# Layer 1's depthwise convolution in blocks of 4 rows by 28 columns instead of 2 rows by 56

## The chip, the cores and the metric

One core of one Trainium2 chip runs the whole kernel. The metric is device microseconds of one execution, as the median of the runs. Engines are called by the profile's names: PE (TensorE, matmuls), PEld (its weight loads), DVE (VectorE), ACT (ScalarE), POOL (GpSimd), SP (SyncE, which here only issues DMA transfers).

## The reference

Two layers on 32 images of 96 channels, 56 x 56 pixels, float32.

```
# layer 0
h = depthwise_conv(x, conv_w 7x7, pad 3) + conv_b
h = layernorm over the 96 channels, * ln_g + ln_b
h = gelu(h @ w1 + b1) @ w2 + b2            # 96 -> 384 -> 96, per pixel
x = h * layer_scale + x
# layer 1, on x
x = silu(depthwise_conv(x, conv_w 5x5, pad 2) + conv_b);  xs = x as [96, 3136]
dts, Bs, Cs = x_proj_w @ xs                # 6, 4 and 4 rows
delta = softplus(dt_w @ dts + dt_b)
log_dA = max(delta * A, log 1e-9);  P = exp(cumsum(log_dA))        # along the pixels, 4 states
hs = P * cumsum(delta * Bs * xs / max(P, 1e-9))
y = sum over the states(hs * Cs) + xs * Ds
```

## The kernel before

Images are taken in 8 groups of 4. The layers run one after the other; layer 0 writes its result x1 to DRAM, layer 1 reads it from there.

**Convolution as matmuls (both layers).** A padded image lies in `xpad`, channels on partitions. "Turns" transpose windows of it into `win`: a window is a block of whole padded rows, here 2, laid out on the partitions (layer 1: 2 x 60 = 120), and `win` holds it for every channel, image and block row. A block of 2 x 56 = 112 outputs is then a sum over KT windows of (taps matrix) x (window): the taps of one channel are banded matrices, prepared on the host, loaded by DMA as the stationary operand; the moving operand is that channel's 4 images x 28 blocks = 112 columns. Layer 1 has KT2 = 3, so 3 matmuls per channel (two instructions each in the trace, since they are fp32), 24 "conv" units of 4 channels per group, each in two pieces. ACT copies a unit's PSUM bank to `conv`. "Back" units transpose `conv` (pixels on partitions) to 128 rows (32 channels x 4 images) x 448 pixels, 4 transposes of 112 columns each, and ACT applies bias and SiLU into `xs`.

**Layer 0.** While group g goes through normalisation, up and down projections in 28 units of 448 pixels, the windows of g+1 are turned beside it; the convolution of g+1 then runs by itself. The last step of a unit is `residual` (L421): DVE adds `ps_down`, the bias and the original pixels into `x1o`, and SP stores `x1o` to DRAM (L279). PE's `down` two units later waits for `x1_done`.

**Layer 1.** A group has 7 bands of 448 pixels (8 rows), 3 tiles of 128 rows and 4 states: S = 84 steps of one tile and state, 12 to a band. A step on DVE is two scans (L1115, L1140) and a product (L1128). POOL makes `u` (L1040) and multiplies by `c_rows` (L1054), PE sums over the states (L1363), ACT makes `d_a` (L1220, L1226). Beside this, the next band's `delta` is prepared: `project` (L1337), `xd` (L1193), stored to DRAM and read back as `b_rows` and `c_rows`, `delta_rows` (L1350), `z_log` on ACT (L1209, L1211, L1202), `delta` on DVE (L1106).

The next group's turns (L1308, 24 units of 15 transposes) and conv units (L1315) are laid beside the steps by an order written out in `units` and `schedule`: one piece or one turn a step up to step 71, the first eight steps all turns, then conv, conv, turn, and from step 56 only conv. Back units come in bursts at steps 35 (3), 60 (7), 72 (8) and 0 of the next group (3); at a burst ACT loads the SiLU table and, behind it, the old table. All front work takes turns in two PSUM banks, and a unit waits until the one two before it is kept by ACT. Group 0's front work runs ahead of everything ("EARLY"). Every engine's order is that of its program; there is no other planner. SP's queue holds all loads: slabs of x1 (32 channels of one image) into three thirds of `xpad` (L911), taps in three slots (L920), `b_rows`, `c_rows`, stores. Each waits for its slot, and what is behind it in the queue waits too. The groups are iterations of a hardware loop.

## Time and profile before

| | |
|---|---|
| median of 3 runs | 3963.23 us (3962.03 to 3977.51) |
| the profiled execution, its own time | 3967.54 us |
| its span, first to last instruction | 3965.7 us |
| mean granted clock of PE | 0.936 |
| busy: PE, DVE, ACT, POOL | 3632.9, 3026.1, 2572.0, 2459.8 us |
| layer 1's convolution matmuls (L1315) | 4608 instructions |

A row of an engine's groups gives busy time, the mean of one instruction and, behind the bar, the idle time just before them and what ended it. Instructions overlap at their ends, so busy times of neighbours add up to a little more than the time that passes; from start to start is what one costs. "issue" is time in which the engine waited for nothing that the profile shows.

### The profile page before, as it was taken

What the parts mean: (1) busy time and instruction counts of PE and PEld (TensorE: products, weight loads), DVE (VectorE), ACT (ScalarE), POOL (GpSimd) and SP (SyncE); (2) the same over time, 40 slices, a digit from 0 to 9 for tenths busy, and PEclk for the clock granted to TensorE, in tenths of its full rate; (3) what the DMA queues carried; (4) which work ended last, traced back from release to release, by engine and by line L of the source; (5) the groups of instructions that cost most, each with busy time, mean ns of one, the idle gap of its engine ahead of it and who ended that gap; (6) DMA issues with size and microseconds to landing.
All of it is one profiled execution on the core that took longest, in us unless ns stands there. A gap on an engine that the chain in (4) does not pass through costs nothing.

```text
span 3965.7 us, 71069 instructions
## 1 busy us (share of the span) xinstructions
PE 3632.9 (92%) x22358; PEld 2638.3 (67%) x22358; DVE 3026.1 (76%) x3888; ACT 2572.0 (65%) x4292; POOL 2459.8 (62%) x2298
## 2 busy tenths in 40 slices
PE   6999999999999999997899898998989989989876
PEld 6888797978788787877666465664655646556422
DVE  3675748475766758481299899998999989999999
ACT  1463818173654628175688787887887888878865
POOL 0362717163543627171287888878887888888898
PEclk9999999999999999998889898998999989989887
DMA  7546374746555474526566464664656646555322
GB/s 223 170 130 221 95 252 101 250 104 205 143 168 177 114 239 98 185 71 151 138 176 172 128 180 129 173 180 122 186 135 166 174 118 184 151 158 169 100 79 64
DMA packets 383733, 612.75 MB, mean 155 GB/s; under 512 B 199967, under 2 KB 324152, under 8 KB 383048
## 3 DMA queue, kind: packets, MB, share of 16 engines
q1 hardware_dynamic: 383336, 607.74, 54.4%
q8 instruction: 214, 3.51, 0.4%
q14 instruction: 183, 1.50, 0.1%
HBM read 527.35 MB, written 80.28 MB: 153 GB/s over the span
## 4 chain that ended last, share of the span: by engine, by line
PE 40%; issue 6%; ACT 3%; POOL 2%; DVE 2%; DMA 0%; DVEq 0%; ACTq 0%; POOLq 0%
PE ps_front L1315 12%; PE ps_y L1363 12%; PE ps_front L1308 4%; PE ps_prep L1337 4%; PE ps_y L1360 3%; PE ps_prep L1350 3%; PE ps_front L1328 2%; DVE h L1140 1%; POOL h L1054 1%; POOL u L1040 1%; DVE ps_q L1115 1%; ACT win L1177 1%; ACT d_a L1226 1%; ACT xs L1184 1%; POOL dxs L1028 1%
## 5 line engine op out<-in xcount | busy, mean ns | idle before, releaser
L322 POOL TENSOR_TENSOR h_low<-act_h,h_high 128x448 fp32r<-128x448 f32 x448 | 597.7, 1353 | 724.5 <-ACT h_high L521 724.2
L516 ACT ACTIVATE act_h<-ps_up,b 128x448 f32<-128x448 f32 x672 | 408.7, 633 | 728.1 <-PE ps_up L634 727.9
L1054 POOL TENSOR_TENSOR h<-h,c_rows 128x448 f32<-128x448 f32 x672 | 728.1, 1084 | 219.5 <-DVE h L1140 141.2
L1363 PE MATMUL ps_y<-h,ident 128*128 128x448 f32 x1344 | 704.8, 612 | 104.9 <-POOL h L1054 92.0
L1040 POOL TENSOR_TENSOR u<-dxs,b_rows 128x448 f32<-128x448 f32 x672 | 762.1, 1134 | 51.9 <-DMA bc_dram<-xd 37.6
L1115 DVE TENSOR_TENSOR_SCAN ps_q<-d_a,q_last,ps_q 128x450 f32<-128x450 f32 x576 | 661.2, 1148 | 0.2 <-ACT d_a L1226 0.2
L1140 DVE TENSOR_TENSOR_SCAN h<-d_a,h_last,ps_q 128x449 f32<-128x449 f32 x576 | 647.0, 1123 | 0.0
L1315 PEld LDWEIGHTS ps_front<-win,taps 120*112 120x112 f32 x4608 | 537.3, 187 | 143.9 <-issue 140.3
L607 PE MATMUL ps_stage<-win,taps 124*112 124x112 f32 x6144 | 608.2, 261 | 2.7 <-DVE w_low L369 2.7
L607 PEld LDWEIGHTS ps_stage<-win,taps 124*112 124x112 f32 x6144 | 607.9, 178 | 3.2 <-DVE w_low L369 2.8
L1220 ACT ACTIVATE d_a<-delta,log_eps,a_neg 128x448 f32<-128x448 f32 x672 | 503.4, 750 | 71.8 <-DVE h L1140 52.9
L1315 PE MATMUL ps_front<-win,taps 120*112 120x112 f32 x4608 | 542.5, 271 | 7.1 <-ACT win L1177 3.7
L1363 PEld LDWEIGHTS ps_y<-h,ident 128*128 128x128 f32 x1344 | 230.8, 202 | 373.2 <-POOL h L1054 207.7
L427 DVE TENSOR_TENSOR conv<-ps_stage,bias_row 112x448 f32<-112x448 f32 x192 | 179.6, 935 | 350.8 <-PE ps_stage L607 350.8
L1128 DVE SCALAR_TENSOR_TENSOR ps_q<-ps_q,u 128x449 f32<-128x449 f32 x672 | 409.4, 609 | 42.3 <-POOL u L1040 42.0
L1226 ACT ACTIVATE d_a<-d_a 128x448 f32<-128x448 f32 x672 | 388.3, 578 | 8.3
L316 POOL TENSOR_TENSOR ln_rstd<-ln_var,minus_half 112x7 f32<-112x7 f32 x128 | 202.7, 1583 | 285.4 <-DVE ln_var L404 281.2
L1177 ACT ACTIVATE conv<-ps_front 112x448 f32<-112x448 f32 x192 | 182.3, 949 | 215.4 <-PE ps_front L1315 215.4
L630 PE MATMUL ps_up<-hn_high,w_high 96*128 96x448 f32 x672 | 259.0, 385 | 38.1 <-DVE hn_low L414 24.9
L1308 PEld LDWEIGHTS ps_front<-ident,x1pad 32*120 32x120 f32 x2880 | 190.0, 138 | 135.1 <-issue 133.4
L1028 POOL TENSOR_TENSOR dxs<-delta,xs 128x448 f32<-128x448 f32 x168 | 190.9, 1136 | 139.5 <-DVE delta L1106 139.5
L1106 DVE SCALAR_TENSOR_TENSOR delta<-ps_prep,z_log 128x448 f32<-128x448 f32 x168 | 103.6, 617 | 216.3 <-ACT z_log L1202 210.4
(83 smaller groups left out, 6190.8 us busy)
## 6 DMA issues: line engine op xcount, KB each, us to landing
taps<-in_t_dram SPq DMA_DIRECT2D x192, 896.0 KB, 5.1
taps<-in_t_dram SPq DMA_DIRECT2D x192, 672.0 KB, 4.7
b_rows<-bc_dram SPq DMA_DIRECT2D x224, 224.0 KB, 3.0
c_rows<-bc_dram SPq DMA_DIRECT2D x224, 224.0 KB, 3.2
xres<-in_x_dram SPq DMA_DIRECT2D x224, 168.0 KB, 2.5
x_dram<-x1o SPq DMA_DIRECT2D x224, 168.0 KB, 2.0
x1pad<-x_dram SPq DMA_DIRECT2D x96, 392.0 KB, 5.8
out_dram<-y SPq DMA_DIRECT2D x168, 224.0 KB, 2.5
```

The lines of the kernel that those rows point to most:

```text
L322: nc.gpsimd.tensor_tensor(h_low[u % 2][:, t, :], act_h[u % 2][:, t, :], h_high[u % 2][:, t, :], ALU.subtract).then_inc(h_low_ready[t], 1)
L516: nc.scalar.activation(act_h[u % 2][:, t, :], ps_up[t][:, 0:BT], ACT.Gelu, bias=b1[:, t:t + 1]).then_inc(gelu_done, 1)
L607: mm = nc.tensor.matmul(ps_stage[q % 2][0:TOK, c * BLOCKS:(c + 1) * BLOCKS], taps[q % SLOTS1][0:WIN1, c, k, :], win[:, q * CQ + c, :, k:k ...
L1040: nc.gpsimd.tensor_tensor(u[s % U_SLOTS][:, 0:BT], dxs[:, t, :], b_rows[n][:, :], ALU.mult).then_inc(u_done, 1)
L1054: nc.gpsimd.tensor_tensor(total, total, c_rows[n][:, :], ALU.mult).then_inc(hc_done, 1)
L1115: nc.vector.tensor_tensor_scan(q_bank(s, BT + 2), d_a[s % DA_SLOTS][:, :], no_q.broadcast_to([128, BT + 2]), q_first[:, 0:1] if b == 0 els ...
L1128: nc.vector.scalar_tensor_tensor(q_bank(s, BT + 1), q_bank(s, BT + 1), 1.0, u[s % U_SLOTS][:, :], ALU.min, ALU.mult).then_inc(gated, 1)
L1140: nc.vector.tensor_tensor_scan(h[:, s % H_SLOTS, :], d_a[s % DA_SLOTS][:, 0:BT + 1], q_bank(s, BT + 1), first, ALU.mult, ALU.add).then_inc ...
L1220: nc.scalar.activation(d_a[s % DA_SLOTS][:, 0:BT], delta[:, t, :], ACT.Relu, bias=log_eps[:, 0:1], scale=a_neg[:, t, n:n + 1]).then_inc(cl ...
L1226: nc.scalar.activation(d_a[s % DA_SLOTS][:, 0:BT], d_a[s % DA_SLOTS][:, 0:BT], ACT.Exp, bias=LOG_EPS).then_inc(d_a_ready, 1)
L1315: mm = nc.tensor.matmul(bank[i][0:TOK, c * BLOCKS:(c + 1) * BLOCKS], taps[n % SLOTS2][0:WIN2, c, w, :], win[cb % 2][:, k * CQ + c, :, w:w ...
L1363: nc.tensor.matmul(total, ident[:, :], h[:, s % H_SLOTS, 0:BT], start=False, stop=(n == N - 1)).then_inc(y_added, 1)
```

## The change

A block of layer 1's convolution becomes 4 rows x 28 columns, still 112 outputs. It is read from a padded half image of 32 columns, so a window is 4 x 32 = 128 values, and two windows (KT2 = 2) hold the 8 rows that 5 taps over 4 rows need. `win` has the same size: 15 windows for each of two halves instead of 30. The moving operand is 4 images x 2 halves x 14 block rows. The halves overlap by the columns that both need; layer 0 writes both, with the zeros at the image's left and right edge, so x1 in DRAM has shape [images x channels, 2, 56, 32], and a slab load copies whole rows. Turns: still two per image, 15 transposes each, of 128 columns instead of 120. Back units: still 4 transposes, their results woven together by rows of 28. The host makes other taps (`patched`), 448 KB a load instead of 672.

```diff
-COLS2 = W + 2 * PAD2
-WIN2 = ROWS * COLS2
-KT2 = (ROWS + K2 - 1) // ROWS
-NWIN2 = (H + 2 * PAD2) // ROWS
+PATCH_ROWS, PATCH_COLS = 4, W // 2
+PCOLS = PATCH_COLS + 2 * PAD2
+SEEN = PCOLS - PAD2
+WIN2 = PATCH_ROWS * PCOLS
+KT2 = (PATCH_ROWS + K2 - 1) // PATCH_ROWS
+ROW_BLK = H // PATCH_ROWS
+ROW_WIN = (H + 2 * PAD2) // PATCH_ROWS
+NWIN2 = 2 * ROW_WIN
+BAND_ROWS = BT // W
+BAND_BLK = BAND_ROWS // PATCH_ROWS
...
-        x1o = [sb(f"x1o{i}", [C, BT]) for i in range(2)]
+        x1o = [sb(f"x1o{i}", [C, 2, BAND_ROWS, PCOLS]) for i in range(2)]
...
-                sp.wait_ge(x1_done, g * UNITS + u + 1)
-                sp.dma_start(x1[ds((g * GI + u // BANDS) * C, C), (u % BANDS) * BT:(u % BANDS + 1) * BT],
-                             x1o[u % 2][:, :]).then_inc(x1_stored[u % 2], 16)
+                sp.wait_ge(x1_done, (g * UNITS + u + 1) * 2)
+                rows = slice(u % BANDS * BAND_ROWS, (u % BANDS + 1) * BAND_ROWS)
+                sp.dma_start(x1[ds((g * GI + u // BANDS) * C, C), :, rows, :].rearrange("c f h w -> c f (h w)"),
+                             x1o[u % 2][:, :, :, :].rearrange("c f h w -> c f (h w)")).then_inc(x1_stored[u % 2], 16)
...
+            for i in range(2):
+                nc.gpsimd.memset(x1o[i][:, 0, :, 0:PAD2], 0.0).then_inc(prepared, 1)
+                nc.gpsimd.memset(x1o[i][:, 1, :, SEEN:PCOLS], 0.0).then_inc(prepared, 1)
...
-                nc.vector.scalar_tensor_tensor(x1o[u % 2][:, :], ps_down[u % 2][0:C, 0:BT], b2[:, 0:1],
-                                               xres[u % 2][:, :], ALU.add, ALU.add).then_inc(x1_done, 1)
+                total = ps_down[u % 2][0:C, 0:BT].rearrange("c (h w) -> c h w", w=W)
+                res = xres[u % 2][:, :].rearrange("c (h w) -> c h w", w=W)
+                for f, seen in enumerate((slice(0, SEEN), slice(W - SEEN, W))):
+                    nc.vector.scalar_tensor_tensor(x1o[u % 2][:, f, :, PAD2 * (1 - f):PAD2 * (1 - f) + SEEN],
+                                                   total[:, :, seen], b2[:, 0:1], res[:, :, seen],
+                                                   ALU.add, ALU.add).then_inc(x1_done, 1)
...
-        xpad = sb("x1pad", [C, H + 2 * PAD2, COLS2])
+        xpad = sb("x1pad", [C, 2, H + 2 * PAD2, PCOLS])
...
-                sp.dma_start(xpad[rows, PAD2:PAD2 + H, PAD2:PAD2 + W],
-                             x1img[ds((f * GI + k % GI) * C + CB * (k // GI), CB), :, :]
-                             ).then_inc(slab_ready[k % SLABS], 16)
+                sp.dma_start(xpad[rows, :, PAD2:PAD2 + H, :].rearrange("c f h w -> c f (h w)"),
+                             x1[ds((f * GI + k % GI) * C + CB * (k // GI), CB), :, :, :
+                                ].rearrange("c f h w -> c f (h w)")).then_inc(slab_ready[k % SLABS], 16)
...
-                    pixels = xpad[rows, :, :].rearrange("p r w -> p (r w)")
+                    pixels = xpad[rows, p, :, :].rearrange("c h w -> c (h w)")
                     for w in range(TW2):
                         mm = nc.tensor.transpose(bank[i][0:WIN2, w * CB:(w + 1) * CB],
-                                                 pixels[:, (p * TW2 + w) * WIN2:(p * TW2 + w + 1) * WIN2],
-                                                 ident[rows, rows])
+                                                 pixels[:, w * WIN2:(w + 1) * WIN2], ident[rows, rows])
...
-                                win[cb % 2][:, k * CQ + c, :, w:w + IMG_BLK],
+                                win[cb % 2][:, k * CQ + c, :, :].rearrange("p i (f r) -> p (i f) r",
+                                                                           f=2)[:, :, w:w + ROW_BLK],
...
-                for j in range(BLKS):
-                    mm = nc.tensor.transpose(bank[i][:, j * TOK:(j + 1) * TOK],
-                                             conv[:, b * BLKS + j, t * 128:(t + 1) * 128], ident[0:TOK, 0:TOK])
+                pixels = bank[i][:, 0:BT].rearrange("p (r o f j) -> p r o f j", r=BAND_BLK, o=PATCH_ROWS, f=2)
+                for r in range(BAND_BLK):
+                    for f in range(2):
+                        mm = nc.tensor.transpose(pixels[:, r, :, f, :],
+                                                 conv[:, f * ROW_BLK + b * BAND_BLK + r, t * 128:(t + 1) * 128],
+                                                 ident[0:TOK, 0:TOK])
...
+def patched(w):
+    t = np.zeros((C, KT2 * PATCH_ROWS, PCOLS, PATCH_ROWS, PATCH_COLS), np.float32)
+    for o in range(PATCH_ROWS):
+        for j in range(PATCH_COLS):
+            t[:, o:o + K2, j:j + K2, o, j] = w
+    t = t.reshape(QUNITS, CQ, KT2, WIN2, TOK).transpose(0, 3, 1, 2, 4)
+    return np.ascontiguousarray(t)
```

## Rows read from the trace of the kernel before

**Rows 1.** The page's slices: busy tenths of DVE in 40 equal slices

```profile
DVE  3675748475766758481299899998999989999999
```

**Rows 2.** Busy time by stretches: a layer 0 stretch, the lead-in, the last group

```profile
core 0: us, PE busy (x) PEld busy (x) DVE busy (x) ACT busy (x) POOL busy (x), PEclk, DMA share, GB/s
1040.00:1120.00 80.00, 77.12 (x424) 60.20 (x423) 64.65 (x97) 66.27 (x120) 57.42 (x42) 1.00 0.42 100
...
1840.00:1920.00 80.00, 71.82 (x708) 66.89 (x708) 0.00 (x0) 43.94 (x48) 0.00 (x0) 0.93 0.77 189
...
3840.00:3920.00 80.00, 57.69 (x101) 17.95 (x102) 80.00 (x97) 52.72 (x91) 71.21 (x74) 0.84 0.26 77
```

**Rows 3.** DVE's timeline over one group of layer 1: start, us, engine, line

```profile
2721.42 1.16 DVE L1115 TENSOR_TENSOR_SCAN ps_q<-d_a,q_first,ps_q 128x450 f32<-128x450 f32 x1 [1.74 <-issue]
...
2783.15 0.62 DVE L1106 SCALAR_TENSOR_TENSOR delta<-ps_prep,z_log 128x448 f32<-128x448 f32 x1 [1.71 <-ACT z_log L1202]
...
2852.08 0.62 DVE L1106 SCALAR_TENSOR_TENSOR delta<-ps_prep,z_log 128x448 f32<-128x448 f32 x1 [2.70 <-ACT z_log L1202]
...
2924.05 0.62 DVE L1106 SCALAR_TENSOR_TENSOR delta<-ps_prep,z_log 128x448 f32<-128x448 f32 x1 [2.70 <-ACT z_log L1202]
...
2959.19 0.62 DVE L1106 SCALAR_TENSOR_TENSOR delta<-ps_prep,z_log 128x448 f32<-128x448 f32 x1 [2.00 <-ACT z_log L1202]
...
2974.05 1.16 DVE L1115 TENSOR_TENSOR_SCAN ps_q<-d_a,q_first,ps_q 128x450 f32<-128x450 f32 x1 [1.67 <-issue]
```

**Rows 4.** Waits of the same group, 2724 to 2976: total, times, longest

```profile
DVE delta L1106 <- ACT z_log L1202: 11.4, 6, 2.7
...
DVE ps_q L1128 <- POOL u L1040: 6.5, 3, 3.7
```

**Rows 5.** PE's timeline in the lead-in

```profile
1838.17 4.66 PE L1315 MATMUL ps_front<-win,taps 120*112 120x112 f32 x24 [1.23 <-ACT win L1177]
...
1847.68 2.58 PE L1315 MATMUL ps_front<-win,taps 120*112 120x112 f32 x24
1850.19 1.06 PE L1308 MATMUL ps_front<-ident,x1pad 32*120 32x32 f32 x15
1851.39 2.58 PE L1315 MATMUL ps_front<-win,taps 120*112 120x112 f32 x24
...
1919.21 13.03 PE L1315 MATMUL ps_front<-win,taps 120*112 120x112 f32 x120
1933.96 4.17 PE L1315 MATMUL ps_front<-win,taps 120*112 120x112 f32 x24 [1.73 <-DMA taps<-in_t_dram]
```

**Rows 6.** SP's timeline: issue of slabs at the lead-in's start and in a group

```profile
1813.50 4.32 SPq L911 DMA_DIRECT2D x1pad<-x_dram  x3
...
2901.80 5.14 SPq L911 DMA_DIRECT2D x1pad<-x_dram  x3
```

**Rows 7.** ACT's timeline at the start of the lead-in

```profile
1825.93 0.21 ACT L1263 ACTIVATE a_neg<-a_neg 128x12 f32<-128x12 f32 x1 [11.80 <-DMA a_neg<-in_a_logs_dram]
```

**Rows 8.** ACT's timeline of the group of rows 3, ahead of three bursts

```profile
2827.84 0.97 ACT L1177 ACTIVATE conv<-ps_front 112x448 f32<-112x448 f32 x1 [2.17 <-PE ps_front L1315]
...
2899.78 0.97 ACT L1177 ACTIVATE conv<-ps_front 112x448 f32<-112x448 f32 x1 [0.95 <-PE ps_front L1315]
...
2940.22 0.95 ACT L1177 ACTIVATE conv<-ps_front 112x448 f32<-112x448 f32 x1 [0.93 <-PE ps_front L1315]
```

**Rows 9.** PE's timeline of that group: its start, and behind the burst at step 60

```profile
2729.05 2.74 PE L1328 MATMUL ps_front<-ident,conv 112*128 112x112 f32 x12 [5.70 <-issue]
...
2906.98 2.53 PE L1315 MATMUL ps_front<-win,taps 120*112 120x112 f32 x12
```

**Rows 10.** Groups by line over the whole span, DVE in layer 0

```profile
L421 DVE SCALAR_TENSOR_TENSOR x1o<-ps_down,b,xres 96x448 f32<-96x448 f32 x224 | 150.7, 673 | 77.1 <-DMA xres<-in_x_dram 46.0 <-PE ps_down L651 30.8
...
L404 DVE TENSOR_SCALAR ln_var<-ln_ss 112x7 f32<-112x7 f32 x128 | 25.4, 198 | 4.4
```

**Rows 11.** The page's DMA issues: count, KB each, median us to landing

```profile
taps<-in_t_dram SPq DMA_DIRECT2D x192, 672.0 KB, 4.7
...
x1pad<-x_dram SPq DMA_DIRECT2D x96, 392.0 KB, 5.8
```

**Rows 12.** Groups by line, the group from 2724 to 2976

```profile
L1328 PE MATMUL ps_front<-ident,conv 112*128 112x112 f32 x84 | 14.8, 330 | 11.0 <-issue 5.7 <-ACT xs L1184 5.2 <-ACT conv L1177 0.2
```

More of the change, by code:

```diff
@@ L100 @@
 assert TILES == CBS and GI * CB == 128
+assert PATCH_ROWS * PATCH_COLS == TOK and WIN2 == 128 and TURNS2 == 2 and TW2 == ROW_WIN
 def window_copy(win, ps_stage, n):
@@ L219, in layer0 @@
         TURN = {BANDS * (i - 1) + 3 + k: i * TURNS1 + 2 * k for i in range(1, GI) for k in range(TURNS1 // 2)}
-        PREPARED = 5
+        EDGES = 4
+        PREPARED = 5 + EDGES
         last = groups - 1
@@ L639, in down @@
                 if u >= 2:
-                    pe.wait_ge(x1_done, g * UNITS + u - 1)
+                    pe.wait_ge(x1_done, (g * UNITS + u - 1) * 2)
                 for t in range(FS):
@@ L716, in layer1 @@
 def layer1(nc, groups, x1, t2, consts, out):
-    x1img = x1.rearrange("r (h w) -> r h w", h=H)
     bc = nc.dram_tensor("bc_dram", (BANDS, N, 2, GI, BT), F32, kind="Internal").ap()
@@ L800, in layer1 @@
         CONSTS = 16 * 6
-        BORDERS = 4
+        BORDERS = 2
         PREPARED = 4 + TILES + 1 + DA_SLOTS + U_SLOTS
@@ L1088, in _ @@
         def _(dve):
-            for border in (xpad[:, 0:PAD2, :], xpad[:, PAD2 + H:, :],
-                           xpad[:, PAD2:PAD2 + H, 0:PAD2], xpad[:, PAD2:PAD2 + H, PAD2 + W:]):
+            for border in (xpad[:, :, 0:PAD2, :], xpad[:, :, PAD2 + H:, :]):
                 nc.vector.memset(border, 0.0).then_inc(xpad_zero, 1)
@@ L1457, in lay_out @@
         "cb1": i["L0_conv_conv_b"],
-        "t2": banded(i["L1_conv_conv_w"][:, 0], K2),
+        "t2": patched(i["L1_conv_conv_w"][:, 0]),
         "xproj": xproj, "dtw": dtw, "one_rows": one_rows,
@@ L1465, in program @@
 def program(nc, groups, a, out):
-    x1 = nc.dram_tensor("x1_dram", (IMAGES * C, L), F32, kind="Internal").ap()
+    x1 = nc.dram_tensor("x1_dram", (IMAGES * C, 2, H, PCOLS), F32, kind="Internal").ap()
     layer0(nc, groups, a["x"], a["t1"], a, x1)
```

## The prediction

> **What bounds the kernel now.** I read the page's slices first [rows 1]: up to the slice with a 1, some 46% of the span, it is layer 0, and VectorE (DVE) is busy by turns; behind it, in layer 1, DVE is at 8 and 9 tenths. The table by stretches says it in numbers [rows 2]: in a layer 0 stretch between two convolutions TensorE (PE) is busy 77.1 of 80 us and DVE 64.7, so PE sets the pace; from 1840 to 1920 us DVE does nothing at all, because layer 1 first has to convolve group 0 (the lead-in), and only PE and ScalarE (ACT) work; in the last group, which has no convolution beside it, DVE is busy 80.0 of 80 and PE 57.7.
>
> Then DVE's timeline in one of the seven layer 1 groups that convolve ahead [rows 3]. The first scan of one group starts at 2721.42 and that of the next at 2974.05: 252.6 us. The waits listed there are the ones that matter: 1.71, 2.70, 2.70 and 2.00 us for `z_log`, in bands 1, 3, 5 and 6. The wait table of the group [rows 4] has 11.4 us for `z_log` and 6.5 us for `u`. About 20 us of the 252.6 are idle on DVE with the starts of the loop body; nothing faster than about 232 is to be had while DVE's own work stands.
>
> `z_log` comes at the end of a chain: transposes back (L1328), SiLU, projection (L1337), `xd`, delta rows (L1350), three activations. PE runs it in the same queue as the convolution pieces, one piece in nearly every step. So a lighter piece counts where PE is behind. That it is behind is seen on ACT, which waited 2.17, 0.95 and 0.93 us for a convolution bank shortly before the bursts of SiLUs at steps 35, 60 and 72 [rows 8].
>
> **The convolution's matmuls.** KT2 goes from 3 to 2, so a unit of four channels goes from 24 matmul instructions to 16 (each fp32 matmul is two), and a piece (half a unit) from 12 to 8. All keep 112 columns in and 112 out. At full clock 24 of them take from 1847.68 to 1850.19, 2.51 us, 0.105 each [rows 5]; most of the 8 removed are worth slightly less than that mean, which holds the start of a unit: I take 0.8 us for a unit, 0.4 for a piece. At half the clock a unit takes 4.66 us [rows 5] and a piece 2.53 [rows 9], so there a third is 1.5 and 0.8 us.
>
> **Lead-in, convolutions.** 24 units, 16 of them alternating with a turn (a unit of window transposes). The pair repeats after 3.71 us (1847.68 to 1851.39) [rows 5]. ACT needs about 2 us of it, so PE still sets a pair of 2.9 us: the whole third is gained. 21 units at full clock give 21 x 0.8 = 16.8 us; three ran at half clock (4.66; another like it; 4.17) and give 4.5. Sum 21.3. Against it: the 24 turns now load 128 columns in place of 120, by 8 in 120 at most 0.07 of 1.06 us, 1.7 us in all. In the last eight units only taps matter to the DMA: before, five ran without a stop and the last waited 1.73 us for its taps [rows 5]. Taps shrink from 672 to 448 KB, as the units do, but a load's fixed part doesn't; with three slots I leave 2 us for it. Net 17.6 us.
>
> **Lead-in, the first slabs.** Three slab loads hold SP's queue for 4.32 us [rows 6], and the small constants are behind them: ACT waited 11.80 us, to 1825.93, for `a_neg` [rows 7], and keeps no window before that. A slab was 32 channels x 56 rows of 224 bytes; it becomes 64 runs of 7168 bytes, 17% more bytes. It now takes 5.8 us to land, against 4.7 for 672 KB of taps in 5376-byte runs [rows 11]. So a slab costs less than those taps, about 4 us, and is issued as fast as they are. I take 4.5 us for the start (0 if latency is all, 8 if the queue is). The lead-in gains 22.1 us in all.
>
> **Steady groups.** In each, PE loses 48 pieces x 0.4 = 19 us of work and gets 24 turns x 0.07 = 1.7 more. What comes out depends on the four waits.
> Band 1 (1.71 us): six pieces run between the group's start and this `z_log`, with PE never idle; 2.4 us saved exceeds the wait. Gain 1.7.
> Band 3 (2.70): ACT waited 2.17 us for PE ahead of the burst [rows 8], and four pieces follow it, 1.6 us. The sum, 3.8, exceeds the wait. Gain 2.7.
> Band 5 (2.70): 0.95 us ahead of the burst [rows 8], then one piece at half clock (0.8) and three at full (1.2). Gain 2.9, more than the `z_log` wait, since part of the waits for `u` just ahead of it goes too. These are from `c_rows`, whose load stands in SP's queue behind the three next slabs (5.14 us of issue [rows 6]) and behind a taps load; it is the chain of `z_log` that is late next, so no more than 2.9 counts.
> Band 6 (2.00): no pieces follow the burst at step 72; only the 0.93 us ahead of it. Gain 1.0.
> Band 0's waits begin with the loop's start: PE stands 5.70 us with nothing in the profile to wait for [rows 9], and then has eight turns and no convolution: slightly worse, 0.3. The `c_rows` behind a slab there land earlier, but DVE would then wait for `z_log` instead.
> Sum 8.0 us a group, seven groups: 56 us. The last group has no convolution and keeps its time.
>
> **Layer 0.** The one `x1o` instruction on 448 elements becomes two on 240. It takes 673 ns, and a 7-element instruction 198 [rows 10]. From these two, 240 elements take 449 ns, two of them 898: 0.225 us more. Only the elements more (32) would be 0.035. I take 0.15 as neighbours overlap, 34 us of DVE in 224 units. Behind it on DVE are the next chunk's normalisation and `hn_low`, for which PE waits in places; PE waits too for `x1_done`, a unit late. But PE sets the pace and DVE has 15 us free in 80 [rows 2], so I let one seventh through, 5 us (bounds 0 and 0.225 x 224 = 50). The store becomes 192 runs of 1024 bytes instead of 96 of 1792, under the same unit; four more fills on GpSimd at the start and two fewer on DVE are well under 1 us. Nothing for them; uncovered, they would be 1.
>
> **What no row shows: strided access by PE.** The transposes back write PSUM in runs of 28 with jumps, where they wrote 112 in a row, and the convolution reads eight runs of 14 instead of four of 28. All matmuls in the trace write contiguous runs. The 84 transposes of a group take 14.8 us [rows 12]. Below: no change. Above: twice, 0.15 us each, of which some is under the SiLUs: 7 us a group and 6 in the lead-in. Nearest are the convolution's own reads, in four runs, which cost no more per column than others; I take 0.
> The Trainium skill ("PSUM — Partial Sum Buffer", Specifications) says that any non-contiguous access pattern slows matmuls significantly. No row here has one on the output. By it the transposes would be at the upper end or past it. It is the ground for the third rival, whose price comes from rows.
>
> **Sum.** 3967.5 (profiled execution: 3965.7 of span, 1.8 around it) - 22.1 - 56 + 5 = 3894.4. That execution was 4.3 us above the median of the runs shown, 3963.2, so I say 3890.
>
> **Rivals.**
> 1. The clock takes it back. The last group, where PE has the least to do, has a granted clock of 0.84, against 1.00 in the stretch of layer 0 [rows 2]. A PE that catches up will wait more often for GpSimd's `h` and run stretches at 1.2 instead of 2.4 GHz. For it: 2.53 us for a piece after the burst [rows 9]. Against: each piece leaves 0.4 us more room to catch up in, and waits on PE alone cost nothing. If half the steady gain goes: 3890 + 28 = 3918.
> The Trainium skill ("TensorE: Matmul & The Clock Gate", "A second HAM failure mode: psum-queue depth-cycling") says that frequent small idle times between groups of matmuls make the clock fall and rise; the 0.84 agrees in kind.
> 2. Layer 0's second instruction is exposed on PE's path: 50 us instead of 5, 3935. For it: DVE to PE waits exist; against: 15 us free in 80.
> 3. On the other side: strided reads make a convolution matmul dearer. At 1.5 times the 0.105 us (0.157) the gain is zero; that is the point from which it decides. At twice, a unit costs 0.8 us more than before, a piece 0.4. PE, late already in four bands of seven, becomes the bound: 19 us of pieces and 7 of transposes a group, 7 x 26 = 182, 19 + 6 in the lead-in, 5 in layer 0, 212 in all: up to 4175.
> 4. The change doesn't reach DVE: the bursts on ACT, not PE, made `z_log` late, and the steady gain is 0 to 1.5 a group. With the lead-in and layer 0: 3967.5 - 22.1 + 5 - 4.3 = 3946, or 3936.
> 5. All waits but the loop's start go (17 us a group): 3890 - 7 x 9 = 3827. Against: band 0's start and the bursts' table loads stay.
>
> **Numbers.** Forecast as told 0.60; rival 1 0.12; rival 2 0.08; rival 3 0.07; rival 4 0.08; rival 5 0.05. Half a per cent (20 us, 3943) is about what a measurement of this kernel can tell. The forecast and rivals 1, 2 and 5 are faster (0.85), half of rival 4 is (0.04), the other half within half a per cent. Of rival 3, 0.02 are transposes doubled and nothing else, 3890 + 7 x 7 + 6 = 3945, also within. So faster 0.89, same 0.06, slower 0.05. Range 3850 to 3938: it leaves out rivals 3 and 5 and most of 4 (0.18 in all), and the ends of my own terms (lead-in 15 to 28, groups 5 to 11, layer 0 0 to 20) are within it.
>
> **What would show it.** Convolution matmuls x3072 instead of 4608 at the same mean; lead-in from PE's first transpose to the first `delta` about 22 us shorter; 244 to 245 us from one group's first scan to the next; waits for `z_log` down from 11.4 us to 4 or 5; last group 231 us still; layer 0's unit time unchanged within 0.05 us; slabs landing in about 4 us. The prediction is wrong if the mean of L1315 or L1328 rises, if the granted clock in the bands falls below 0.9, or if another wait takes the place of `z_log`.

## The result, and the profile after

The changed kernel takes 3929.1 us (median of 4 runs, 3926.7 to 3930.4), the kernel before 3966.4 us on the same chip. The ratio is 0.990, 95% interval 0.989 to 0.992: faster, by 37 us. The forecast was 3890 us, so the gain is just over half of the 73 us forecast. The profiled execution took 3928.4 us, with a span of 3926.5.

First the groups by line, for the instructions that the change touches: busy time and mean ns of one, then the idle time before them.

```profile
L1327 PE MATMUL ps_front<-win,taps 128*112 128x112 f32 x3072 | 387.3, 274 | 5.9 <-ACT win L1190 3.7 <-DMA taps<-in_t_dram 1.2
L646 PE MATMUL ps_up<-hn_high,w_high 96*128 96x448 f32 x672 | 260.6, 388 | 55.4 <-DVE hn_low L426 40.6 <-issue 14.6
L436 DVE SCALAR_TENSOR_TENSOR x1o<-ps_down,b,xres 96x240 f32<-96x240 f32 x448 | 186.3, 454 | 85.3 <-DMA xres<-in_x_dram 53.6 <-PE ps_down L667 31.0
L1343 PE MATMUL ps_front<-ident,conv 112*128 112x112 f32 x672 | 101.9, 290 | 76.6 <-ACT xs L1197 63.1 <-issue 11.7 <-ACT conv L1190 1.6
```

The convolution's instructions are 3072 as announced, and the transposes back, which now write with jumps, take 290 ns in the mean where they took 330 [rows 12]; that is a matter of the clock they ran at, not of the jumps (see rival 3 below). The adds of layer 0 take 186.3 us in place of 150.7 [rows 10], and `hn_low` keeps PE waiting for 40.6 us (24.9 in the same view of before).

Then where layer 0 ends, and the lead-in: two rows of DVE's timeline, one of ACT's, three of PE's.

```profile
1841.99 0.84 DVE L436 SCALAR_TENSOR_TENSOR x1o<-ps_down,b,xres 96x240 f32<-96x240 f32 x2 [1.14 <-PE ps_down L667]
...
1857.48 0.21 ACT L1276 ACTIVATE a_neg<-a_neg 128x12 f32<-128x12 f32 x1 [10.29 <-DMA a_neg<-in_a_logs_dram]
...
1879.57 1.80 PE L1327 MATMUL ps_front<-win,taps 128*112 128x112 f32 x16
1881.30 1.11 PE L1321 MATMUL ps_front<-ident,x1pad 32*128 32x32 f32 x15
1882.49 1.80 PE L1327 MATMUL ps_front<-win,taps 128*112 128x112 f32 x16
...
1972.19 1.16 DVE L1128 TENSOR_TENSOR_SCAN ps_q<-d_a,q_first,ps_q 128x450 f32<-128x450 f32 x1 [3.10 <-ACT d_a L1239]
```

Before, the last `x1o` began at 1809.67 us and the first scan at 1959.73. So layer 0 lost 32.3 us, and the lead-in from the one to the other shrank from 150.1 to 130.2. A pair of unit and turn repeats after 2.92 us instead of 3.71 [rows 5].

Last, DVE's timeline in the group that answers to [rows 3]: all its waits.

```profile
2708.84 1.16 DVE L1128 TENSOR_TENSOR_SCAN ps_q<-d_a,q_first,ps_q 128x450 f32<-128x450 f32 x1 [1.73 <-issue]
2723.89 1.16 DVE L1128 TENSOR_TENSOR_SCAN ps_q<-d_a,q_first,ps_q 128x450 f32<-128x450 f32 x1 [0.15 <-ACT d_a L1239]
2732.43 0.63 DVE L1141 SCALAR_TENSOR_TENSOR ps_q<-ps_q,u 128x449 f32<-128x449 f32 x1 [3.73 <-POOL u L1054]
2734.27 0.62 DVE L1119 SCALAR_TENSOR_TENSOR delta<-ps_prep,z_log 128x448 f32<-128x448 f32 x1 [1.20 <-ACT z_log L1215]
2744.59 0.62 DVE L1119 SCALAR_TENSOR_TENSOR delta<-ps_prep,z_log 128x448 f32<-128x448 f32 x1 [4.46 <-ACT z_log L1215]
2750.86 0.62 DVE L1119 SCALAR_TENSOR_TENSOR delta<-ps_prep,z_log 128x448 f32<-128x448 f32 x1 [0.34 <-ACT z_log L1215]
2772.74 0.62 DVE L1119 SCALAR_TENSOR_TENSOR delta<-ps_prep,z_log 128x448 f32<-128x448 f32 x1 [0.33 <-ACT z_log L1215]
2902.18 0.63 DVE L1141 SCALAR_TENSOR_TENSOR ps_q<-ps_q,u 128x449 f32<-128x449 f32 x1 [0.34 <-POOL u L1054]
2906.64 0.62 DVE L1119 SCALAR_TENSOR_TENSOR delta<-ps_prep,z_log 128x448 f32<-128x448 f32 x1 [1.22 <-ACT z_log L1215]
2954.57 1.16 DVE L1128 TENSOR_TENSOR_SCAN ps_q<-d_a,q_first,ps_q 128x450 f32<-128x450 f32 x1 [1.70 <-issue]
```

Read it from the bottom: the `z_log` waits of bands 3 and 6 are gone, band 5's is 1.22 us where it was 2.70, and band 1's is 0.33. In band 0 the second of three is now 4.46 us, where 1.19 stood before, and the third 0.34, where there was none. All in all DVE waits 7.5 us for `z_log` in this group, 11.4 before [rows 4]. From one group's first scan to the next (2708.84 to 2954.57) it is 245.7 us in place of 252.6. Group 0 went from 256.5 to 244.8.

### The profile page after: what moved, and what is told of

Read it like the earlier page. It is cut to its first block and busy times, and to the rows that moved or that the text cites. A ratio compares the mean times of both kernels' runs of the same rounds, so it can differ in the third digit from the quotient of the medians.

```text
span 3926.5 us, 68379 instructions
## 1 busy us (share of the span) xinstructions
PE 3527.5 (90%) x20822; PEld 2507.0 (64%) x20822; DVE 3057.5 (78%) x4110; ACT 2571.6 (65%) x4292; POOL 2467.4 (63%) x2302
## 5 line engine op out<-in xcount | busy, mean ns | idle before, releaser
L1379 PE MATMUL ps_y<-h,ident 128*128 128x448 f32 x1344 | 733.5, 635 | 149.4 <-POOL h L1068 104.4
L1379 PEld LDWEIGHTS ps_y<-h,ident 128*128 128x128 f32 x1344 | 239.0, 210 | 417.6 <-POOL h L1068 273.0
L1327 PEld LDWEIGHTS ps_front<-win,taps 128*112 128x112 f32 x3072 | 383.1, 190 | 150.1 <-issue 146.4
L1327 PE MATMUL ps_front<-win,taps 128*112 128x112 f32 x3072 | 387.3, 274 | 5.9 <-ACT win L1190 3.7
L646 PE MATMUL ps_up<-hn_high,w_high 96*128 96x448 f32 x672 | 260.6, 388 | 55.4 <-DVE hn_low L426 40.6
L1321 PEld LDWEIGHTS ps_front<-ident,x1pad 32*128 32x128 f32 x2880 | 213.9, 150 | 145.5 <-issue 144.1
L1190 ACT ACTIVATE win<-ps_front 128x480 f32<-128x480 f32 x192 | 205.1, 1069 | 82.6 <-PE ps_front L1321 78.3
L650 PE MATMUL ps_up<-hn_low,w_high 96*128 96x448 f32 x672 | 252.8, 376 | 0.0
```

What stands on the lines that cost most here:

```text
L1327: mm = nc.tensor.matmul(bank[i][0:TOK, c * BLOCKS:(c + 1) * BLOCKS], taps[n % SLOTS2][0:WIN2, c, w, :], win[cb % 2][:, k * CQ + c, :, :].r ...
L1379: nc.tensor.matmul(total, ident[:, :], h[:, s % H_SLOTS, 0:BT], start=False, stop=(n == N - 1)).then_inc(y_added, 1)
```

## The experiments

Marks used below: "last `x1o`" is the start of the last row of layer 0's residual on DVE; "group" is the time from a group's first scan to the next one's; "band" the time from its first scan to that of the next, 12 scans later. A band without waits takes 33.0 us.

### Layer 0: is it the second add?

**One add split in two, in the kernel before**

```diff
-                nc.vector.scalar_tensor_tensor(x1o[u % 2][:, :], ps_down[u % 2][0:C, 0:BT], b2[:, 0:1],
-                                               xres[u % 2][:, :], ALU.add, ALU.add).then_inc(x1_done, 1)
...
+                for seen in (slice(0, 28), slice(28, W)):
+                    nc.vector.scalar_tensor_tensor(put[:, :, seen], total[:, :, seen], b2[:, 0:1],
+                                                   res[:, :, seen], ALU.add, ALU.add).then_inc(x1_done, 1)
```

> The kernel before, with layer 0's residual as two VectorE instructions of 8 rows by 28 columns (224 elements each) in place of one of 448; the output tile, its store and all of layer 1 stay as before. Theory A (the second instruction's fixed cost stands on layer 0's loop nearly in full, since VectorE is what its units wait for): two instructions take about 2 x 0.44 us where one took 0.67, so +0.20 us in each of 448 units; the last x1o comes 25 to 32 us later than 1809.67 us, the layer 1 stages don't move, total about +28 us (3990 to 3998 beside 3966). Rival B (layer 0's loss came from SP's dearer store of 16 runs per row and the later xres loads): nothing here, within 5 us of before, last x1o within 3 us of 1809.67. Rival C (it came from the clock, with the changed tiles as its cause): nothing here either.

Measured: 3989.4 us, ratio to before 1.007 (1.005 to 1.009).

```profile
L425 DVE SCALAR_TENSOR_TENSOR x1o<-ps_down,b,xres 96x224 f32<-96x224 f32 x448 | 178.7, 437 | 79.6 <-DMA xres<-in_x_dram 47.1 <-PE ps_down L655 31.7 <-issue 0.2
...
1832.46 0.81 DVE L425 SCALAR_TENSOR_TENSOR x1o<-ps_down,b,xres 96x224 f32<-96x224 f32 x2 [1.18 <-PE ps_down L655]
```

DVE's adds take 28.0 us more than before [rows 10], the last `x1o` came 22.8 us late, and layer 1 did not move (groups 1 to 5 take 252.2 to 252.7). The split alone makes most of the 32.3 us, so theory A holds in kind; 22.8 us and 3989.4 are a little under the 25 to 32 us and the 3990 that it asked for at least.

**Layer 0 put back, the halves made by layer 1's slab loads**

```diff
-                sp.dma_start(xpad[rows, :, PAD2:PAD2 + H, :].rearrange("c f h w -> c f (h w)"),
-                             x1[ds((f * GI + k % GI) * C + CB * (k // GI), CB), :, :, :
-                                ].rearrange("c f h w -> c f (h w)")).then_inc(slab_ready[k % SLABS], 16)
+                for half, seen in enumerate((slice(0, SEEN), slice(W - SEEN, W))):
+                    left = PAD2 * (1 - half)
+                    sp.dma_start(xpad[rows, half, PAD2:PAD2 + H, left:left + SEEN],
+                                 x1img[ds((f * GI + k % GI) * C + CB * (k // GI), CB), :, seen]
+                                 ).then_inc(slab_ready[k % SLABS], 16)
...
```

> The changed kernel with its layer 0 put back as before (one add of 448 elements, contiguous store, x1 as plain images); the two overlapping halves are made by layer 1's slab loads instead, two DMAs for each slab with runs of 120 bytes. Theory A (layer 0 lost through the second add): the last x1o comes at 1810 us again, 32 us sooner than in the changed kernel. Theory D (layer 1's gain is the third matmul of each channel, not the contiguous slabs): groups 1 to 6 stay at 246 us and group 0 at 245, the lead-in stays near 130 us or is up to 6 us longer from the dearer slab issue (6 issues of some 1.4 us instead of 3 of 0.64), total 3897 to 3905. Rival E (the steady gain came from the contiguous slabs: less queueing of DMAs, c_rows and b_rows sooner): groups 1 to 6 go back to 252 us or more, total 3940 or more.

Measured: 3898.2 us, ratio 0.984 (0.982 to 0.987). The last `x1o` is at 1803.0 us, the lead-in 133.2 us, the groups 242 to 249. So the steady gain doesn't need contiguous slabs: runs of 120 bytes leave groups of 246 us on the mean. The lead-in is 3 us longer for them.

**The store with one run for each channel**

```diff
-                sp.dma_start(x1[ds((g * GI + u // BANDS) * C, C), :, rows, :].rearrange("c f h w -> c f (h w)"),
-                             x1o[u % 2][:, :, :, :].rearrange("c f h w -> c f (h w)")).then_inc(x1_stored[u % 2], 16)
+                sp.dma_start(x1[ds((g * GI + u // BANDS) * C, C), u % BANDS, :, :, :].rearrange("c f h w -> c (f h w)"),
+                             x1o[u % 2][:, :, :, :].rearrange("c f h w -> c (f h w)")).then_inc(x1_stored[u % 2], 16)
...
```

> The changed kernel with x1 kept by bands in DRAM, so that layer 0's store of a unit has one run of 2 KB for each channel in place of two of 1 KB, and layer 1's slabs are read in runs of 1 KB in place of 7 KB, by two DMAs each; the two adds stay where the change has them. Splitting the add alone cost 23.2 of layer 0's 32.3 us. Theory Q (the rest is the two instructions' own length, 240 elements and another shape instead of 224, not the store): last x1o within 4 us of 1842. Rival R (the rest is the store with two runs for each channel): last x1o at 1832 to 1837. Groups of layer 1 stay at 246 us in both, the lead-in gets 1 to 4 us longer; total 3926 to 3934 by theory Q, 3920 to 3926 by rival R.

Measured: 3922.4 us, ratio to before 0.990 (0.987 to 0.992), last `x1o` at 1832.8 us, 9.2 sooner than in the changed kernel and where the split add alone had put it. Below, its adds, one of its stores on SP, and, as the last row, a store of the changed kernel:

```profile
L435 DVE SCALAR_TENSOR_TENSOR x1o<-ps_down,b,xres 96x240 f32<-96x240 f32 x448 | 186.3, 454 | 78.2 <-DMA xres<-in_x_dram 45.6 <-PE ps_down L666 31.9
...
1053.38 0.35 SPq L287 DMA_DIRECT2D x_dram<-x1o  x1
```

```profile
1043.83 0.59 SPq L288 DMA_DIRECT2D x_dram<-x1o  x1
```

The adds are as long as in the changed kernel, 454 ns, and DVE's wait for `xres` is 45.6 us again where the changed kernel has 53.6 and before had 46.0 [rows 10]. `xres` is issued on SP right behind the store, and the store with two runs takes 0.59 us to issue in place of 0.35. Rival R holds, with a caution: four kernels with one and the same layer 0 ended it from 1803.0 to 1809.7, so the size of the 9 us is not far above the scatter. The direction is firmer, since the other runs sort the same way: with two early adds and the store in one run, layer 0 ended at 1832.5 and 1832.8 (two kernels), with the store in two runs at 1842.0 to 1847.1 (four), and the wait for `xres` was 45.6 and 47.1 us against 49.2 to 53.6.

**The adds placed later**

```diff
-                if u > 0:
-                    residual(g, u - 1)
                 for c, step in ln_at[u]:
                     if step in (2, 3, 4):
                         ln(g, c, step)
+                if u > 0:
+                    residual(g, u - 1)
```

> The changed kernel with layer 0's two adds of a unit placed after the last layer norm steps of that unit on VectorE instead of before them; nothing is left out. Theory A1 (VectorE is so full in layer 0's unit stages that any time added to it counts, wherever it stands): unit stages stay at 151 to 153 us, last x1o at about 1842 us, total within 6 us of 3929. Rival A2 (what counts is that the adds stand ahead of the layer norm steps that the next back transposes wait for): unit stages shorten by 3 us or more, last x1o by 15 to 30 us.

Measured: 3890.4 us, ratio 0.981 (0.978 to 0.984), 39 us less than the changed kernel. A1 falls: VectorE was not simply full. The adds stood in front of the normalisation for which the next units wait: PE's wait for `hn_low` went from 40.6 to 25.7 us, and the one for `conv` ahead of the transposes back (`ps_back`) from 27.0 to 12.9. The last `x1o` came 36 us sooner, more than the 15 to 30 that A2 gave it. The same edit in the kernel before:

> The kernel before, with layer 0's one add of a unit placed after the unit's last layer norm steps; nothing else. The changed kernel with the late adds took 3890 us, its last x1o at 1806 us where the changed kernel has 1842. Theory M (what costs is work of VectorE that stands ahead of the layer norm steps, so a single late add is worth its own 0.67 us in part too): the last x1o comes 15 to 30 us sooner than 1809.67, total 3937 to 3952. Rival N (only the second add was in the way, and one add is hidden where it stands): last x1o within 4 us of 1806, total 3960 to 3967. Layer 1 unchanged in both.

Measured: 3925.7 us, ratio 0.991 (0.988 to 0.994); rival N falls. Theory M has the direction, but 36 us on the last `x1o` and the total are beyond its numbers too. The last `x1o` of both, first that of the changed kernel with late adds:

```profile
1805.85 0.84 DVE L436 SCALAR_TENSOR_TENSOR x1o<-ps_down,b,xres 96x240 f32<-96x240 f32 x2 [1.14 <-PE ps_down L667]
```

```profile
L421 DVE SCALAR_TENSOR_TENSOR x1o<-ps_down,b,xres 96x448 f32<-96x448 f32 x224 | 150.8, 673 | 40.0 <-DMA xres<-in_x_dram 23.4 <-PE ps_down L651 16.6
...
1773.35 0.68 DVE L421 SCALAR_TENSOR_TENSOR x1o<-ps_down,b,xres 96x448 f32<-96x448 f32 x1 [1.30 <-PE ps_down L651]
```

The two edits add up, as the last `x1o` of all the kernels with the two stores as they were shows:

| | one add, us | two adds, us | what the second add and the store cost |
|---|---|---|---|
| early | 1803.0 to 1809.7 (4 kernels, mean 1807.2) | 1842.0 to 1847.1 (4, mean 1843.8) | +36.6 |
| late | 1773.4, 1772.5 | 1805.9, 1811.5 | +35.8 |
| late against early | -34.3 | -35.1 | |

(For pairs of adds it is the row of the first of the two. 1811.5 is from a profiled execution that was the slowest of its kernel's four, the last run below.) Two things follow. The change's layer 0, second add and longer store together, costs about 36 us wherever it stands. And the early place costs 35 us with one add or two. That is not the add's length, which is 673 ns in both places, but most likely its waits: late, those for `xres` and `ps_down` are 40.0 us in all, early 77.1 [rows 10]; with two adds they are 47.1 and 85.3.

### Layer 1: the count of matmuls

**Three matmuls for each channel again**

```diff
-                        for w in range(KT2):
+                        for k3, w in enumerate((0, 0, 1)):
...
-                                start=(w == 0), stop=(w == KT2 - 1))
+                                start=(k3 < 2), stop=(k3 != 1))
```

> The changed kernel, with the first conv matmul of each channel of layer 1 issued twice (the second overwrites the first), so that there are three matmuls for each channel as before; patches, contiguous slabs and layer 0 stay as changed. Theory D (the count of conv matmuls is the gain of layer 1): the convs of the lead-in cost 0.75 us a channel pair more, the lead-in goes from 130 back to 148 us, groups 1 to 6 from 246.0 back to 252 us or so, group 0 from 245 to 256, total about 3929 + 18 + 6 x 6.6 + 11 = 3998 (3985 to 4005). Rival E (contiguous slabs are the steady gain): the lead-in alone moves, total 3945 to 3950. Layer 0 stays at 1842 us in both.

Measured: 4011.5 us, ratio to before 1.013 (1.008 to 1.018), the slowest of all. PE's timeline in the lead-in has before's unit of 2.58 us [rows 5] back, with 24 instructions:

```profile
1888.20 2.58 PE L1327 MATMUL ps_front<-win,taps 128*112 128x112 f32 x24
1890.71 1.12 PE L1321 MATMUL ps_front<-ident,x1pad 32*128 32x32 f32 x15
1891.91 2.58 PE L1327 MATMUL ps_front<-win,taps 128*112 128x112 f32 x24
```

The pair is 3.71 us, as before. The lead-in goes from 130 to 143 us; the rest of the way to 150 is not the count. Bands 5 and 6 go back to 37 to 39 us. Theory D holds for the lead-in and for these bands, and the seven groups together take 59.6 us more than in the changed kernel, all that it had gained there (52.3) and more. Its numbers do not hold: the total is over its 4005, and the groups do not go back to 252. The first two take 245.4 and 249.2 us, the others 254 to 260. The new shape with the old count is worse than the old kernel, and from the fourth group on the difference is mostly in band 0 (43.5 to 44.1 us, 38.9 before). In the first group band 0 took 35.3 us; with it goes another granted clock, the last number but two in each of these rows:

```profile
1990.30:2025.60 35.30, 29.53 (x183) 17.28 (x184) 32.34 (x40) 31.71 (x50) 26.81 (x28) 0.84 0.40 114
2994.90:3038.70 43.80, 38.01 (x176) 21.36 (x177) 32.67 (x40) 30.26 (x46) 27.07 (x29) 0.62 0.40 109
```

### Band 0: what the clock has to do with it

In the changed kernel band 0 takes 42.6 us where it took 38.9. The table by stretches, changed kernel: band 0, then the part of it with the first turns and the part with the last ones; below them PE's last row with an idle time before it:

```profile
core 0: us, PE busy (x) PEld busy (x) DVE busy (x) ACT busy (x) POOL busy (x), PEclk, DMA share, GB/s
2708.80:2751.60 42.80, 38.20 (x174) 21.13 (x175) 32.84 (x40) 30.16 (x46) 27.34 (x29) 0.62 0.39 111
...
2721.10:2731.70 10.60, 10.60 (x87) 6.74 (x86) 7.45 (x9) 9.15 (x15) 1.45 (x2) 0.98 0.48 139
2731.70:2752.20 20.50, 20.50 (x74) 11.41 (x73) 13.77 (x18) 14.01 (x23) 17.59 (x19) 0.50 0.48 135
```

```profile
2717.01 1.01 PE L1343 MATMUL ps_front<-ident,conv 112*128 112x112 f32 x4 [2.60 <-ACT xs L1197]
```

For 20.5 us PE is busy all the time at a granted clock of 0.5 (1.2 GHz), and DVE idles a third of it. PE has not been idle since 2717.0, 14.7 us ahead of the fall. Before, the whole band had 0.76.

**Windows of 120 values**

```diff
-                        mm = nc.tensor.transpose(bank[i][0:WIN2, w * CB:(w + 1) * CB],
-                                                 pixels[:, w * WIN2:(w + 1) * WIN2], ident[rows, rows])
+                        mm = nc.tensor.transpose(bank[i][0:NARROW, w * CB:(w + 1) * CB],
+                                                 pixels[:, w * WIN2:w * WIN2 + NARROW], ident[rows, rows])
...
```

> The changed kernel with layer 1's windows cut from 128 to 120 of their values, as wide as before's: turns, window copies and conv matmuls take 120; the last 8 values of each window are left out of the convolution, so the output is not the reference's. Theory F (band 0 lost 3.4 us because the turns' weights are 128 columns wide and PE falls behind there at a low clock): band 0 of groups 1 to 6 goes from 42.5 us at a mean clock of 0.62 back to about 39 us at 0.76, groups of about 242 us, total about 3905. Rival G (where the low stretches fall in band 0 is set by when work arrives around the group's start, and 8 columns don't move that): band 0 stays within 1.5 us of 42.5 or moves without an order, total 3920 to 3932.

Measured: 3918.3 us, ratio to before 0.988 (0.984 to 0.991). Two groups of this one execution:

```profile
2216.30:2258.20 41.90, 37.18 (x173) 20.33 (x174) 32.62 (x39) 30.07 (x46) 27.07 (x29) 0.62 0.38 114
2461.70:2499.50 37.80, 31.79 (x183) 18.27 (x184) 32.56 (x40) 29.66 (x46) 25.27 (x27) 0.78 0.41 120
```

The same code took 41.9 us in one group at 0.62, and 37.8 in the next at 0.78; four of the six groups were of the first kind. Theory F's number fails: width doesn't settle which it is, and rival G, by which the stretches move without an order, is nearer. But the length of band 0 mostly goes with its clock. In the run with the halo in the slab loads three groups stand on the same line: 38.4 us at 0.72, 41.0 at 0.67, 42.5 at 0.62. It is no strict rule: another group of that run took 45.5 us at 0.61, and one of the run with the one-run store 42.5 at 0.66. And that the two go together doesn't show which of them is the cause.

**More work for PE around the group's start**

```diff
+                if s >= S - 8 or s < 2:
+                    for _ in range(2):
+                        nc.tensor.matmul(ps_y[r % Y_SLOTS][0:STEPS, 0:BT], zeros[:, :], h[:, s % H_SLOTS, 0:BT],
+                                         start=False, stop=False)
                 nc.tensor.matmul(total, ident[:, :], h[:, s % H_SLOTS, 0:BT],
```

> The changed kernel with two matmuls of zeros (12 output rows, 448 columns) added ahead of each y matmul of the last 8 steps and the first 2 of a group of layer 1; the result is the same. PE has 1.2 to 2.3 us of idle time in these steps. Theory O (the low granted clock in band 0 comes from PE's thin work around the group's start, and with it the 9.5 us that band 0 is over its 33.0): the mean clock of band 0 goes from 0.62 to 0.75 or more and band 0 from 42.5 to 36 to 40 us, total 3890 to 3915. Rival P (the clock falls again over the turns of 32 rows by themselves, whatever came before): band 0 keeps 0.60 to 0.65 and 42 us or more, total 3929 to 3940.

Measured: 3968.5 us (10 runs), ratio to before 1.000 (0.999 to 1.002), so 39 us slower than the changed kernel.

```profile
2703.20:2724.30 21.10, 21.10 (x50) 5.76 (x50) 19.58 (x24) 15.93 (x29) 19.27 (x19) 1.00 0.34 103
2724.30:2754.30 30.00, 24.41 (x123) 10.52 (x121) 20.42 (x23) 16.18 (x24) 14.06 (x16) 0.89 0.24 69
2754.30:2774.70 20.40, 20.40 (x74) 11.52 (x74) 12.94 (x17) 14.07 (x23) 13.94 (x15) 0.50 0.46 133
```

```profile
2736.32 1.01 PE L1343 MATMUL ps_front<-ident,conv 112*128 112x112 f32 x4 [5.59 <-ACT xs L1197]
```

The clock was 1.00 ahead of the group's start. It was 0.50 from 2733.8 to 2740.5, around the idle time of 5.59 us, 1.00 again from 2740.7 to 2754.2, over the first turns, and then 0.50 for 20.4 us over the last ones all the same. Rival P is right about the fall, though not in its numbers. Theory O got nearly the mean clock it asked for (0.73 of 0.75) and a band 0 of 49.4 us: the added work stands in PE's queue ahead of the transposes back, which most likely makes them late. As a test of what the clock is worth it is spoilt by that. Nor does it rule out that the idle time at the group's start, which it left in place, has to do with the fall some 18 us later.

**Turns for four images at once**

```diff
...
-                    rows = slice(CB * (slab % SLABS), CB * (slab % SLABS) + CB)
-                    pixels = xpad[rows, p, :, :].rearrange("c h w -> c (h w)")
-                    for w in range(TW2):
-                        mm = nc.tensor.transpose(bank[i][0:WIN2, w * CB:(w + 1) * CB],
-                                                 pixels[:, w * WIN2:(w + 1) * WIN2], ident[rows, rows])
+                    pixels = xpad[:, k, :, :].rearrange("c h w -> c (h w)")
+                    a, z = p * TW2, min((p + 1) * TW2, ROW_WIN)
+                    for w in range(a, z):
+                        mm = nc.tensor.transpose(bank[i][0:WIN2, (w - a) * 128:(w - a + 1) * 128],
+                                                 pixels[:, w * WIN2:(w + 1) * WIN2], ident[:, :])
...
```

> The kernel of the run with the halo in the slab loads (3898 us), with layer 1's turns made for 4 images at once: x1pad holds 32 channels of 4 images on 128 partitions, each turn unit is 4 transposes of 128x128 in place of 15 of 32x128, and the slabs are loaded by halves of all four images. Theory H (band 0 is long because PE is late there: 15 transposes of 32 rows take 1.12 us of it at full clock and 1.80 at half clock, and the clock stays low over them): a turn takes 0.5 to 0.8 us, PE is no longer full in band 0, band 0 goes from 42 to 34 to 37 us, groups to 237 to 241 us, total about 3898 - 7 x 6 = 3856 (3840 to 3870). Rival I (band 0's waits are those of the burst of back transposes, xs and delta at its start and not of the turns): groups stay at 244 to 247 us, total 3890 to 3900. Rival J (a slab half of four images comes too late for its first turn): new waits of PE for slabs, groups above 247 us.

Measured: 3866.5 us, ratio 0.975 (0.972 to 0.977), 32 us under the run it builds on (3898.2). First its band 0, then the stretch of its turns:

```profile
2416.60:2453.30 36.70, 26.54 (x93) 13.54 (x94) 32.34 (x40) 29.51 (x46) 26.73 (x28) 0.84 0.51 128
...
2428.60:2444.20 15.60, 14.07 (x54) 7.21 (x54) 11.40 (x15) 14.84 (x25) 9.22 (x10) 1.00 0.58 119
```

A turn takes 0.60 us, PE is no longer full (26.5 of 36.7 us), the clock holds 1.00 over the turns, and band 0 is 36.7 to 37.1 us. Groups 1 to 5 are 242 to 243 us: 5.2 us less in band 0 than in the run it builds on, of which bands 3 and 5 give back 2.2. The total is in theory H's range, though a group gained 3.5 us and not 6; the lead-in, 6 us shorter, gave some of it. Of the slower turn and the lower clock I can't say which share each had: both went together.

### The start of layer 1

**Constants ahead of the slabs**, in the kernel of the last run

```diff
-                if n == SLABS:
+                if n == 0:
```

> The kernel with turns for 4 images at once, and layer 1's small constants loaded ahead of its first slabs instead of after them. Theory K (the start of layer 1 waits for ScalarE's a_neg, whose constants lie behind the slabs in the queue, but PE's first turns wait for the slabs alone, and a_neg is not on the way to the first scan): 2 us slower to 1 us faster than the same kernel without it, since the slabs come later by the constants' issue (6 issues of about 0.45 us). Rival L (the constants' arrival holds up the lead-in): 3 to 5 us faster.

Measured: 3863.7 us against 3866.5 in the same series, the ranges overlapping (3861.8 to 3868.6 and 3864.6 to 3871.4). ACT's timeline:

```profile
1815.72 0.21 ACT L1274 ACTIVATE a_neg<-a_neg 128x12 f32<-128x12 f32 x1 [3.29 <-DMA a_neg<-in_a_logs_dram]
1822.69 2.06 ACT L1188 ACTIVATE win<-ps_front 128x512 f32<-128x512 f32 x2 [6.75 <-PE ps_front L1317]
```

`a_neg` comes 12.9 us sooner (1828.64 in the kernel without the edit), and ACT then waits 6.75 us for PE's first turn. The lead-in goes from 126.9 to 124.7 us. Neither theory's number: the wait moved from one load to the other.

### All together

The last kernel with the single late add:

> The kernel with turns for 4 images at once and the constants first (3864 us; last x1o at 1808), with its single add of layer 0 placed late. By theory M 15 to 30 us sooner (3834 to 3849); by rival N the same within 4 us. Layer 1's groups stay at 241 to 243 us.

Measured: 3830.3 us, ratio 0.966 (0.964 to 0.969), last `x1o` at 1772.5, groups 242 to 244 (the first and the last that convolve ahead 240 and 239). This is the best, 99 us under the changed kernel, and its last `x1o` came 35.5 us sooner than without the late add, over the 15 to 30 of theory M. And with the change's own layer 0 in it:

> As the run before it, but with the change's own layer 0 (two overlapping adds, here late, and contiguous slabs) in place of the halo made by the slab loads. Its layer 0 should end where that of the late adds in the changed kernel did, at 1806 us. If contiguous slabs are worth something once the adds are out of the way, the lead-in is 2 to 4 us shorter and the groups up to 1 us; total 3855 to 3864, so by theory M slower than the run before it and by rival N the same or a little faster.

Measured: 3855.6 us, ratio 0.972 (0.969 to 0.974). The lead-in is 1.6 us shorter and the groups are about the same; layer 0 costs 39 us more in the profile. The profiled execution was the slowest of four, at 3860.4 us; the medians are 25 us apart.

## Why the prediction was wrong

By its own steps, against the profiled executions (3965.7 us of span before, 3926.5 after):

| term | forecast, us | measured, us |
|---|---|---|
| lead-in | -22.1 | -19.9 |
| seven groups | -56 | -52.3 |
| layer 0 | +5 | +32.3 |
| last group | 0 | +0.7 |
| sum | -73 | -39.2 |

**The step that failed is the one for layer 0**: "PE sets the pace and DVE has 15 us free in 80, so I let one seventh through, 5 us". It makes 27 of the 34 us that were missing. DVE's added time was sized well (34 us forecast, 35.6 measured); the share let through was wrong. The split add alone made 28.0 us of adds and 22.8 us of delay, and the changed kernel with a one-run store 35.6 and 23.1: two thirds to four fifths, not one seventh. In a loop from DVE over PE and ACT back to DVE, free time on one engine is the time in which it waits for the others, and doesn't cover work that stands between two links. The prediction's own sign for this term was a unit of layer 0 unchanged within 0.05 us; it grew by 32.3 us in 224 units, 0.14 each. The waits were there to be read before: 24.9 us of PE for `hn_low`, 129.4 us of DVE for `hn_high`. The other part, the store's second run for each channel, was costed at nothing because it lay "under the same unit". The one-run store shows about 9 us for it, most likely through the `xres` load behind it in SP's queue; the scatter of 6.7 us between equal layer 0s leaves its size open. Rival 2, held at 0.08, was what happened, at 32 us instead of 50.

**Lead-in.** The matmuls went as told: 0.79 us a pair (0.8 forecast), and giving back the third matmul put the pair at 3.71 us again. The start gave under 1 us and not 4.5: PE's wait for the first slab hardly moved (9.23 to 9.11 us), so there latency and not the queue is most likely what counts, the low end that the prediction named. Its slab was off too: 448 KB against 392 is 14% more, not 17, and it lands after 5.2 us (median), not about 4.

**Groups.** 6.9 us in place of 8.0 in the group shown; the seven gave 52.3, between them 7.5 on the mean, since group 0 gave more. Bands 1, 3, 5 and 6 gave 10.6 us (8.3 forecast): band 5 alone went from 38.9 to 34.8. Band 0 lost 3.7 us where 0.3 was forecast. There is a wait for `z_log` there of 4.46 us, 3.3 more than before, while PE runs 20.5 us at 1.2 GHz. The prediction's sum for a group had no term for a turn at the lower clock. Its sign for the clock, below 0.9 in the bands, couldn't have told it either: band 0 was at 0.76 before the change. Group 0, whose band 0 had a clock of 0.58 before already, lost nothing there and gained 11.7 us, which is near the 10.6 that the other bands of each group gained. Rivals 4 (0 to 1.5 us a group) and 5 (17) are both out by this.

**Rival 1** has the clock right and the place wrong: band 0 gave back 3.7 of 10.6 us, at the lower clock, but in a stretch in which PE was 100% busy, and not in one in which it had caught up and waited. The Trainium skill ("TensorE: Matmul & The Clock Gate", "A second HAM failure mode: psum-queue depth-cycling") ties the fall to small idle times between groups of matmuls; around the group's start the trace agrees, with 0.50 from 2707.9 to 2721.4 us and idle times of 1.2, 1.8 and 2.6 us in it. The stretch over the turns has none, nor have the 14.7 us ahead of it, so there the rule doesn't describe the fall.

**Rival 3** is out. The means of 290 against 330 ns can't show it by themselves, because they mix two clocks: of the 672 transposes back, 295 ran wholly at 1.2 GHz before, and 102 after. So eight of them in one piece, at a granted clock of 1.00, first before and then after the change:

```profile
1939.14 0.99 PE L1328 MATMUL ps_front<-ident,conv 112*128 112x112 f32 x8 [1.01 <-ACT conv L1177]
```

```profile
1953.25 0.98 PE L1343 MATMUL ps_front<-ident,conv 112*128 112x112 f32 x8 [1.01 <-ACT conv L1190]
```

At 0.50 eight take 1.75 us in both kernels (at 1954.10 before, at 2712.65 after). The convolution's instruction has 274 against 271 ns, and a unit at full clock takes 0.108 us for each from start to start, against 0.105. The Trainium skill ("PSUM — Partial Sum Buffer", Specifications) would have the transposes slowed significantly; no run here shows that for fp32 in runs of 28.

**Open.** What decides whether the low clock over the turns lasts 20.5 us or 3.4: one execution of one kernel showed both (the one with windows of 120 values). No run took away PE's idle time at the group's start, so what it has to do with the fall stays open too. Whether the turns' own length or the clock does more harm wasn't separated. A third buffer for `xres`, which might take its remaining waits (21.7 and 23.4 us in the two kernels with one late add), wasn't tried.

## What to carry to other kernels

An engine's free time covers added work only if the work stands off the loop that passes through that engine; when its neighbours show waits for it, charge most of the addition (here two thirds to four fifths came through). And compare the mean of an instruction before and after only at the same granted clock. Before pricing an instruction in such a loop, look at what stands in front of it in its queue: moving one add with its waits behind the work that others wait for was worth as much here (35 us) as the whole change to the convolution's matmuls gave back in net. A change that is good in one place and costs in another can often be split: making the overlap in the consumer's loads kept layer 1's gain and gave layer 0 its time back.

## What the hardware showed that I hadn't expected

- PE kept a granted clock of 0.5 for 20.5 us while it was busy all the time, as it had been for 14.7 us before, alternating transposes of 32 rows with full matmuls; with transposes of 128 rows, and less work in all (14.1 us busy in 15.6), the clock held 1.00.
- Four transposes of 128x128 take 0.60 us; fifteen of 32x128, which move 15/16 as many values, take 1.12, both at a clock of 1.00.
- The clock's pattern over the same code can differ from group to group of one execution (0.62 and 0.78), and band 0 was 4 us longer or shorter along with it.
